# A GNN, FFN and Mamba block on one core: decays by halves of the heads, long steps as two, and another order of the steps on all five engines

## The reference, cut to what matters

```python
x = x + relu(elu(gat(relu(mlp2(elu(gat(relu(mlp1(ln(x))))) + res))), adj) + res2)  # part a, then b
x = x + ffn_on_top_rows(ln(x))      # part q: 127 of 256 rows by a router score, up, gelu, down, put back
x = x + elu(masked_gat(ln(x)))      # part g
x = x + mamba2(ln(x))               # part m: 8 heads of 64, one chunk of 256 steps
```

## Time and profile before

| | |
|---|---|
| median of 3 runs | 3752.43 us |
| the runs | 3751.11 to 3752.57 us |
| profiled execution | 3752.41 us, its span 3750.7 us |
| TensorE matmuls busy | 3618.9 us (96%) |
| TensorE weight loads busy | 3158.1 us (84%) |
| VectorE busy | 2973.1 us (79%) |
| ScalarE busy | 2364.2 us (63%) |
| GpSimd busy | 993.9 us (26%) |
| mean granted TensorE clock | 0.985 of full |

### The profile page before, as it was taken

The page is one execution under the profiler, slowest core; times in us unless marked ns, Lnnn a source line. Parts: engine busy times, 40 slices in busy tenths (PEclk is TensorE's granted clock), DMA queues, the critical chain, the costliest instruction groups (busy, mean ns, idle before and its releaser), DMA issues.

```text
span 3750.7 us, 63924 instructions
## 1 busy us (share of the span) xinstructions
PE 3618.9 (96%) x21016; PEld 3158.1 (84%) x21016; DVE 2973.1 (79%) x7729; ACT 2364.2 (63%) x5314; POOL 993.9 (26%) x1821
## 2 busy tenths in 40 slices
PE   6799999999999999999999999999999999999975
...
DMA packets 73763, 126.85 MB, mean 34 GB/s; under 512 B 9984, under 2 KB 64128, under 8 KB 65536
## 3 DMA queue, kind: packets, MB, share of 16 engines
...
...
## 4 chain that ended last, share of the span: by engine, by line
PE 87%; DVE 8%; issue 2%; ACT 1%; POOL 0%; ACTq 0%; DVEq 0%; POOLq 0%
PE A L1199 12%; PE M L1335 7%; PE A L1219 7%; PE Q L1323 6%; PE A L1237 6%; PE A L1188 6%; PE Q L1316 6%; PE M L1369 6%; PE M L1428 6%; PE A L1284 3%; PE A L1246 3%; PE Q L1246 3%; PE Q L1284 3%; PE A L1229 2%; PE M L1357 2%
## 5 line engine op out<-in xcount | busy, mean ns | idle before, releaser
L1199 PE MATMUL A<-w_fc,o1T 128*128 128x256 f32 (+1 forms) x2048 | 454.7, 380 | 3.8 <-ACT o1T L541 3.8
L1199 PEld LDWEIGHTS A<-w_fc,o1T 128*128 128x128 f32 x2048 | 382.9, 189 | 57.8 <-ACT o1T L541 4.0
L433 POOL TENSOR_TENSOR var_m<-mv_m,epsilon 128x2 f32<-128x2 f32 x64 | 12.6, 197 | 1414.7 <-DVE mv_m L813 1414.7
L710 ACT ACTIVATE dec<-cumB,cumcol 128x256 f32<-128x256 f32 (+1 forms) x1024 | 366.2, 443 | 0.0
L1022 DVE SCALAR_TENSOR_TENSOR acc<-M,w_conv,acc 128x255 f32<-128x255 f32 (+2 forms) x768 | 315.0, 470 | 0.0
L1335 PE MATMUL M<-xT_m,w_in 128*128 128x256 f32 x1280 | 297.5, 379 | 0.8 <-DVE tz L1064 0.5
L1219 PE MATMUL A<-h,low 128*128 128x257 f32 (+1 forms) x1024 | 256.4, 395 | 22.9 <-DVE low L854 14.0
L1335 PEld LDWEIGHTS M<-xT_m,w_in 128*128 128x128 f32 x1280 | 237.7, 190 | 32.1 <-DVE tz L1064 2.0
L1323 PE MATMUL Q<-w_down,gsq 128*128 128x256 f32 x1024 | 241.2, 390 | 9.7 <-DVE gsq L995 9.7
L1316 PE MATMUL Q<-selT,w_up 128*128 128x128 f32 x2048 | 249.5, 275 | 0.9 <-ACT selT L646 0.9
L1064 DVE SCALAR_TENSOR_TENSOR tz<-tz,M 128x512 f32<-128x512 f32 x128 | 88.1, 688 | 202.5 <-ACT tz L693 202.5
...
## 6 DMA issues: line engine op xcount, KB each, us to landing
...
```

Source lines behind the costliest of these rows:

```text
L710: last = nc.scalar.activation(dec[:, h, :], columns[:, h, :], ACT.Relu, bias=cumcol[:, i, h:h + 1], scale=-1.0)
L1199: last = nc.tensor.matmul(rows1(half, u, 2), o1T[:, k, u * P:(u + 1) * P], w_fc[:, k, half, 0:D + 2 * i], start=(k == 0), stop=(k == KH - 1))
```

## The change

Five kinds of edits:

- The decays are made by halves of the heads. ScalarE's `m_decay` has four pieces in place of two: dec0 and dec1 of the first four heads, then of the last four, each with four relus and an exp of half the size. VectorE's `m_mix` has four pieces likewise. TensorE's `m_y.0` waits for the first two mixes only, `m_y.1` for all four. `m_scan` may start when the decays of the block before are done, as before.
- Steps of TensorE in two: `q_ffn2`, `m_z`, `m_out` and `a_mlp2` (the last two along their outer loops, as `m_z` is below). They signal when the last part is done, `m_z` after each.
- VectorE's `m_silu` is parted into `m_silu` and `m_silu_bc`.
- GpSimd's `m_dt_log` is parted after the sixth link; both parts stand side by side.
- All five lists are in another order, and the turn begins at another step.

```diff
 STEPS = {
-    "tensor": [('q_gather', 3), ('b_att', 2), ('m_cum_col', 5), ('q_ffn1.0', 3), ('b_res', 2), ('q_ffn1.1', 3), ('a_mlp1.0', 1), ('a_mlp1.1', 1), ('m_xrow', 5), ('m_cb', 5), ('a_fc.0', 1), ('a_fc.1', 1), ('q_ffn2', 3), ('a_bcast', 1), ('m_turn', 4), ('q_scatter', 3), ('m_y.0', 5), ('m_y.1', 5), ('a_att.0', 1), ('g_turn', 3), ('a_att.1', 1), ('g_proj', 3), ('m_out', 5), ('g_bcast', 3), ('m_ss', 5), ('a_uturn', 1), ('m_dt', 4), ('q_route', 2), ('a_mlp2', 1), ('m_z', 4), ('g_pturn', 3), ('b_proj', 1), ('m_xbc_a', 4), ('b_bcast', 1), ('m_xbc_b', 4), ('m_da', 4), ('a_turn', 0), ('g_att', 3), ('b_pturn', 1)],
-    "vector": [('g_stats', 4), ('a_probs', 2), ('g_norm', 4), ('m_y.0', 6), ('a_att', 2), ('m_y.1', 6), ('q_norm', 3), ('g_proj', 4), ('m_sq', 6), ('q_route', 3), ('a_elu_c', 2), ('g_mask', 4), ('m_ms', 6), ('a_uturn', 2), ('g_lrelu', 4), ('m_dt', 5), ('a_norm', 1), ('g_max', 4), ('m_out', 6), ('q_rank', 3), ('m_gate', 5), ('b_proj', 2), ('b_mask', 2), ('b_lrelu', 2), ('b_max', 2), ('g_pturn', 4), ('m_scan', 5), ('m_conv_b.0', 5), ('b_pturn', 2), ('m_conv_b.1', 5), ('g_elu_b', 4), ('m_conv_b.2', 5), ('m_cum_col', 5), ('b_elu_c', 2), ('b_x1', 2), ('q_gelu_a', 3), ('m_silu', 5), ('g_x3', 4), ('q_stats', 2), ('a_stats', 0), ('q_gelu_b', 3), ('m_stats', 4), ('m_cb', 5), ('a_fc', 1), ('m_norm', 4), ('q_ffn2', 3), ('m_mix.0', 5), ('a_fcol', 1), ('m_mix.1', 5), ('q_scatter', 3), ('a_maxima', 1), ('q_x2', 3)],
-    "scalar": [('a_att', 1), ('m_gated', 5), ('a_elu_b', 1), ('g_proj', 3), ('q_route', 2), ('m_dt_exp', 4), ('g_exp', 3), ('a_mlp2', 1), ('m_z', 4), ('b_proj', 1), ('g_pturn', 3), ('m_xbc_a', 4), ('m_xbc_b', 4), ('b_exp', 1), ('g_att', 3), ('b_pturn', 1), ('g_elu', 3), ('q_gather', 2), ('b_att', 1), ('b_elu_b', 1), ('a_turn', 0), ('m_silu', 4), ('q_gelu_a', 2), ('a_mlp1', 0), ('m_decay.0', 4), ('q_gelu_c', 2), ('m_decay.1', 4), ('m_xrow', 4), ('a_factors', 0), ('a_fcol', 0), ('g_turn', 2), ('m_turn', 3)],
-    "gpsimd": [('a_norm', 0), ('q_norm', 2), ('g_norm', 3), ('q_turn', 2), ('m_rms', 5), ('m_dt_log', 4), ('m_da', 4), ('m_turn', 4), ('m_norm', 3), ('m_xrow', 4)],
-    "sync": [('a_load', 0), ('a_residual', 2), ('m_store', 6), ('m_spread', 5)],
+    "tensor": [
+        ("m_cb", 5), ("a_fc.0", 1), ("a_fc.1", 1), ("q_ffn2.0", 3), ("a_bcast", 1), ("m_turn", 4), ("q_ffn2.1", 3),
+        ("m_y.0", 5), ("q_scatter", 3), ("m_y.1", 5), ("a_att.0", 1), ("a_att.1", 1), ("g_turn", 3), ("m_z.0", 4),
+        ("g_proj", 3), ("m_out.0", 5), ("a_uturn", 1), ("g_bcast", 3), ("m_out.1", 5), ("m_ss", 5), ("a_mlp2.0", 1),
+        ("a_mlp2.1", 1), ("m_dt", 4), ("q_route", 2), ("b_proj", 1), ("m_z.1", 4), ("g_pturn", 3), ("b_bcast", 1),
+        ("m_xbc_a", 4), ("m_xbc_b", 4), ("q_gather", 2), ("b_pturn", 1), ("a_turn", 0), ("b_att", 1), ("m_da", 4),
+        ("g_att", 3), ("b_res", 1), ("m_cum_col", 4), ("q_ffn1.0", 2), ("a_mlp1.0", 0), ("a_mlp1.1", 0),
+        ("q_ffn1.1", 2), ("m_xrow", 4),
+    ],
+    "vector": [
+        ("a_probs", 1), ("q_x2", 3), ("g_stats", 3), ("a_att", 1), ("g_norm", 3), ("m_y.0", 5), ("m_y.1", 5),
+        ("a_elu_c", 1), ("g_proj", 3), ("m_sq", 5), ("a_uturn", 1), ("g_mask", 3), ("q_norm", 2), ("g_lrelu", 3),
+        ("m_ms", 5), ("a_stats", 0), ("q_route", 2), ("a_norm", 0), ("g_max", 3), ("m_dt", 4), ("m_out", 5),
+        ("b_proj", 1), ("q_rank", 2), ("m_gate", 4), ("b_mask", 1), ("b_lrelu", 1), ("b_max", 1), ("g_pturn", 3),
+        ("m_conv_b.0", 4), ("b_pturn", 1), ("m_conv_b.1", 4), ("m_scan", 4), ("m_conv_b.2", 4), ("b_elu_c", 1),
+        ("b_x1", 1), ("m_cum_col", 4), ("g_elu_b", 3), ("m_silu", 4), ("m_silu_bc", 4), ("g_x3", 3), ("q_gelu_a", 2),
+        ("m_stats", 3), ("q_stats", 1), ("q_gelu_b", 2), ("m_norm", 3), ("m_cb", 4), ("q_ffn2", 2), ("a_fc", 0),
+        ("a_fcol", 0), ("m_mix.0", 4), ("m_mix.1", 4), ("a_maxima", 0), ("m_mix.2", 4), ("q_scatter", 2),
+        ("m_mix.3", 4),
+    ],
+    "scalar": [
+        ("g_pturn", 3), ("q_gather", 2), ("b_att", 1), ("b_elu_b", 1), ("g_att", 3), ("a_turn", 0), ("g_elu", 3),
+        ("m_silu", 4), ("a_mlp1", 0), ("m_xrow", 4), ("q_gelu_a", 2), ("m_decay.0", 4), ("q_gelu_c", 2),
+        ("m_decay.1", 4), ("m_decay.2", 4), ("m_decay.3", 4), ("a_factors", 0), ("a_fcol", 0), ("m_turn", 3),
+        ("a_att", 0), ("g_turn", 2), ("a_elu_b", 0), ("m_gated", 4), ("g_proj", 2), ("a_mlp2", 0), ("q_route", 1),
+        ("m_dt_exp", 3), ("g_exp", 2), ("b_proj", 0), ("m_z", 3), ("m_xbc_a", 3), ("b_exp", 0), ("m_xbc_b", 3),
+        ("b_pturn", 0),
+    ],
+    "gpsimd": [
+        ("m_da", 5), ("m_turn", 5), ("m_xrow", 5), ("m_norm", 4), ("g_norm", 3), ("q_norm", 2), ("a_norm", 0),
+        ("m_rms", 5), ("q_turn", 2), ("m_dt_log.0", 4), ("m_dt_log.1", 4),
+    ],
+    "sync": [
+        ("m_store", 6), ("a_load", 0), ("a_residual", 2), ("m_spread", 5),
+    ],
 }
...
-            def m_dt_log(b):
-
-                after(S["dt_e_ready"], b)
+            def m_dt_log(b, half):
+
+                if half == 0:
+                    after(S["dt_e_ready"], b)
...
-                for i, link in enumerate(links):
+                for i in ((0, 1, 2, 3, 4, 5), range(6, CHAIN))[half]:
                     if i:
                         pool.wait_ge(S["dt_chain"], nth(b, CHAIN, i))
-                    link().then_inc(S["dt_chain"], 1)
+                    links[i]().then_inc(S["dt_chain"], 1)
+                if half == 0:
+                    return
...
-                act.wait_ge(S["cumcol_ready"], b)
-                act.wait_ge(cum_spread, 16 * b)
-                if not (isinstance(b, int) and b < 2):
-                    act.wait_ge(S["y_ps"], nth(b, 2, 0))
-                dec, columns = ((dec0, cumB), (dec1, cumB[:, :, P:]))[i]
-                for h in range(NH):
-                    last = nc.scalar.activation(dec[:, h, :], columns[:, h, :], ACT.Relu, bias=cumcol[:, i, h:h + 1],
+                half, side = divmod(i, 2)
+                if i == 0:
+                    act.wait_ge(S["cumcol_ready"], b)
+                    act.wait_ge(cum_spread, 16 * b)
+                    if not (isinstance(b, int) and b < 2):
+                        act.wait_ge(S["y_ps"], nth(b, 2, 0))
+                dec, columns = ((dec0, cumB), (dec1, cumB[:, :, P:]))[side]
+                heads = slice(half * NH // 2, (half + 1) * NH // 2)
+                for h in range(heads.start, heads.stop):
+                    last = nc.scalar.activation(dec[:, h, :], columns[:, h, :], ACT.Relu, bias=cumcol[:, side, h:h + 1],
                                                 scale=-1.0)
                 last.then_inc(S["fall_ready"], 1)
-                act.wait_ge(S["fall_ready"], nth(b, 2, i + 1))
-                nc.scalar.activation(dec[:], dec[:], ACT.Exp, scale=-1.0)                    .then_inc(S[("dec0_ready", "dec1_ready")[i]], 1)
+                act.wait_ge(S["fall_ready"], nth(b, 4, i + 1))
+                nc.scalar.activation(dec[:, heads, :], dec[:, heads, :], ACT.Exp, scale=-1.0)\
+                    .then_inc(S[("dec0_ready", "dec1_ready")[side]], 1)
...
+            def m_silu_bc(b):
+                v.wait_ge(S["th_ready"], b)
+                c = acc
...
-                before(v, S["dec1_ready"], b)
+                if not (isinstance(b, int) and b < 2):
+                    v.wait_ge(S["dec1_ready"], nth(b, 2, 0))
...
-                v.wait_ge(S[("dec0_ready", "dec1_ready")[i]], b)
+                half, side = divmod(i, 2)
+                v.wait_ge(S[("dec0_ready", "dec1_ready")[side]], nth(b, 2, half + 1))
                 v.wait_ge(S["cb_ready"], b)
-                dec, c_b = ((dec0, cb[:, None, 0:N]), (dec1, cb[:, None, N:]))[i]
-                nc.vector.tensor_tensor(dec[:], dec[:], c_b.to_broadcast([P, NH, c_b.shape[-1]]), ALU.mult)\
+                heads = slice(half * NH // 2, (half + 1) * NH // 2)
+                dec, c_b = ((dec0, cb[:, None, 0:N]), (dec1, cb[:, None, N:]))[side]
+                nc.vector.tensor_tensor(dec[:, heads, :], dec[:, heads, :],
+                                        c_b.to_broadcast([P, NH // 2, c_b.shape[-1]]), ALU.mult)\
...
-            def q_ffn2(b):
+            def q_ffn2(b, i):
                 pe.wait_ge(S["gl_ready"], b)
-                for m in range(KF):
+                for m in range(i * KF // 2, (i + 1) * KF // 2):
                     last = nc.tensor.matmul(Q0[:, 0:D], gl[:, m, :], w_down[:, m, :], start=(m == 0), stop=(m == KF - 1))
-                last.then_inc(S["yff_ps"], 1)
+                if i:
+                    last.then_inc(S["yff_ps"], 1)
...
-                for i, ps in enumerate((M0, M2)):
-                    if i:
-                        before(pe, S["x4_ready"], b)
-                    for k in (2 * i, 2 * i + 1):
-                        for c in range(KD):
-                            last = nc.tensor.matmul(ps[:, (k - 2 * i) * N:(k - 2 * i + 1) * N],
-                                                    w_in[:, c, Z0 + k * P:Z0 + (k + 1) * P], xT["m"][:, c, :],
```

(47 more changed lines are left out.)

8 lines of the change are left out of this document (3 added, 5 removed).

## The result

The changed kernel takes 3817.1 us (3816.6 to 3817.3) against 3752.5: a ratio of 1.0174, 95% interval 1.0159 to 1.0189. That is slower, as forecast, but by 64.6 us where the forecast had 27, and outside its range. The profiled execution has a span of 3815.5 us.

The account below looks back on a forecast made before the run. TensorE was taken to bound the middle turn (55.80 us); the terms summed to +0.54 us a turn, times 59 +31.9, less 5 at the ends: 3779.3 us. The forecast's own range was 3759 to 3801, the wider one 3745 to 3801.

Parts of the forecast that it names:

- Term 1: At a_att.0: half of q_ffn2 now follows a_bcast, so the wait for VectorE's probabilities goes; -0.42 us a turn.
- Term 5: Around m_y and b_proj: two changes between tile shapes instead of one, and less cover for o2T; +0.09 us a turn.
- Term 3: At a_mlp1.0: TensorE arrives sooner and waits for v1, behind VectorE's chain from m_da; +0.33 us a turn.
- Term 4: At the m_xbc_a tiles: less work covers the gating of z's second half; +0.14 us a turn.
- Term 2: At b_att: only a_turn, not q_gather, covers ScalarE's copy of pT_b; +0.40 us a turn.
- Costed at nothing: GpSimd's m_xrow ahead of m_norm, and the splits' added ScalarE and VectorE instructions: no cost, hidden by slack.
- The ends: Start and end of the kernel: start -1.5 and -3.5 us, end 0 (-7 to +4); -5 us in all.
- A: Rival, faster: b_att's round trip hides, v1 is ready and a_att.0's wait goes; 3723 us, chance 0.14.
- B: Rival, nothing: only b_att waits, -0.02 us a turn; 3746 us, chance 0.13.
- C: Rival, slower still: VectorE's chain decides, a_mlp1.0 or m_y.1 waits 0.5 us more; +1.04 a turn, 3809 us, chance 0.10.

Follow-up runs that it names:

- e4: Kernel before, with VectorE's a_probs writing nothing and TensorE's a_att waiting for low instead: 3742.7 us, ratio 0.9976.
- e6: Kernel before, with TensorE's m_turn moved between m_y.0 and m_y.1: 3778.4 us, ratio 1.0075.
- e2: Changed kernel, with TensorE's m_da before b_att instead of after it: 3789.4 us, ratio 1.0102.
- e7: Kernel before, with ScalarE's b_pturn before its g_att: 3745.0 us, ratio 0.9982.
- e8: e2 with TensorE's m_ss before m_out.1 and ScalarE's q_gelu_a before m_xrow: 3824.3 us, ratio 1.0194.
- e10: e8 with GpSimd's m_norm before its m_xrow, as in the kernel before: 3783.5 us, ratio 1.0085.
- e5: All edits to the steps, but the five lists and lags of the kernel before, split parts side by side: 3767.7 us, ratio 1.0044.
- e9: e2 with m_cum_col behind q_ffn1.1 on TensorE; on VectorE m_scan behind b_x1, m_cum_col behind g_x3: 3794.9 us, ratio 1.0117.

## Why the prediction was wrong, point by point

It named the right place, the right sign and four of the waits, and put the sum at +0.54 us a turn where 1.07 came out. Of the 38 us that the time lies above the forecast, 31 are in the turn and 7 in the ends.

- **Term 1, a_att.0, -0.42: the step that failed.** The wait was 0.22 (e4). The other 0.20 came from m_y's tiles of 64 columns and stays without any wait (e4, e6). The prediction read m_y's natural time as the listed 2.82 less an overlap of 0.16 measured on full tiles; it is 2.75, and 2 x 1.45 when the halves are apart. The weight loads' wait for low holds 0.2 us that is seen before a_att without any late probabilities.
- **Term 5, small, +0.09.** It saw the change of shape in q_scatter's 0.96 us and sized it from that row alone. Two more passes cost 0.30 (e6), by the same count 0.34 in the changed kernel; b_proj and the step before it cost 0.13 more. That b_proj waits for ScalarE's o2T, which ends 0.05 us before it, is read from the rows and wasn't tried. Terms 1 and 5 together were forecast at -0.33, and this part of the turn came to +0.07 (passes +0.34, the wait for the probabilities -0.22, and -0.06 at q_ffn2, which no longer waits for gsq) and b_proj to +0.13: 0.5 us a turn, 31 us, all of the turn's excess; the next two points add 0.13, and the 0.16 that three small steps save takes it away again.
- **Term 3, v1, +0.33:** right in cause, 0.44 in size. e2 confirms the chain from m_da. The changed kernel's VectorE waits for v1's inputs as predicted.
- **Term 4, tiles of m_xbc_a, +0.14:** 0.16.
- **Term 2, b_att, +0.40:** 0.41, with an idle time of 0.24 shown and a distance of 1.28. e2 and e7 confirm it. The Trainium skill's figure beside this term (ScalarE: Activation LUTs, Rules for kernel authors) is for an activation whose bias is a [128,1] pointer operand, which this copy doesn't have; so its 0.73 us was no rival to the row's 0.59.
- **Costed at nothing.** GpSimd's m_norm behind m_xrow: in the changed kernel VectorE's m_norm waits 0.9 us for it and TensorE doesn't, but little slack was left: when e8 makes that wait 2.8 us, TensorE waits for gsq, and in e10 it doesn't. The splits: no wait is seen for them in the new order, 0.27 us a turn in the old (e5).
- **The ends, -5:** the start gave 5.1 us, which is partly luck. The waits for the probabilities shrank as forecast (from 2.98 and 2.89 us to 0.71 and 0.27 in two turns), but other waits grew, and 3.5 of the 5.1 us are matmuls that ran at a higher granted clock. The end, taken at 0 with bounds of -7 to +4, cost 7, and there too it is the clock (0.84 against 0.88) and not the sum of the waits. The prediction had no term for the clock in the ends.
- **Rivals.** A needed the copy to hide, and it didn't. B is excluded by a turn of 56.87. C came out near in time (3809) but not in kind: the wait for v1 cost 0.11 us more than forecast and not 0.5, e9 shows VectorE's chain matched by ScalarE's within 0.2 us, and the excess lies in the passes and in a wait that was smaller than taken.
